# Chosen rows of the last gated layer go to the output by indirect, accumulating transfers

## The reference, cut to what matters

```python
x = x + attn_a(layernorm(x), Wq, Wk, Wv, Wo)            # causal, 16 heads of 16
x = x + ffn(layernorm(x), Wg, Wq, Wk, Wv, Wo)           # gated attention, "layer 1"
x = x + attn_b(layernorm(x), w_qkv, w_out, rel_bias)    # 16 heads of 64, with a bias
x = x + ffn(layernorm(x), Wg, Wq, Wk, Wv, Wo)           # the same gated attention, "layer 3"

def ffn(t):                       # t: 8 x 512 x 256
    gate = sigmoid((t @ Wg)[..., 0])
    _, idx = top_k(gate, 256)                           # 256 of 512 tokens of each sample
    a = take_along_axis(t, idx[..., None], axis=1)
    q, k, v = heads(a @ Wq), heads(a @ Wk), heads(a @ Wv)
    o = merge(softmax(q @ k.T / sqrt(16)) @ v) @ Wo
    out = zeros_like(t)
    out[rows, idx] = o * take_along_axis(gate, idx, axis=1)[..., None]
    return out
```

## Time and profile before

| | |
|---|---|
| median of 3 runs | 2024.09 us (2023.55 to 2024.71) |
| profiled execution | 2022.95 us, span 2020.9 us |
| PE, PE weight loads, VectorE, ACT, GpSimd busy | 98%, 63%, 75%, 57%, 34% |
| granted TensorE clock, share of full speed | 0.998 |
| transfers | 14.9% of 16 engines' time, 49 GB/s of HBM over the span |

### The profile page before, as it was taken

The page is one execution under the profiler, slowest core; times in us unless marked ns, Lnnn a source line. Parts: engine busy times, 40 slices in busy tenths (PEclk is TensorE's granted clock), DMA queues, the critical chain, the costliest instruction groups (busy, mean ns, idle before and its releaser), DMA issues.

```text
span 2020.9 us, 41852 instructions
## 1 busy us (share of the span) xinstructions
PE 1970.7 (98%) x15934; PEld 1264.9 (63%) x15934; DVE 1518.8 (75%) x4803; ACT 1158.5 (57%) x2578; POOL 690.7 (34%) x879
## 2 busy tenths in 40 slices
PE   8999999999999999999999999999999999999998
PEld 6566665666665666656666566655666566666577
DVE  8987767767877778868779687796787967856536
ACT  2455674575637765376644757367663576627642
POOL 5323234242333323433324324234233342313320
PEclk9999999999999999999999999999999999999999
DMA  4001221111201121111211112011120111102200
GB/s 170 2 1 35 78 79 46 46 54 35 84 27 54 46 73 46 45 36 63 74 37 35 54 46 83 29 53 54 42 78 19 61 54 41 68 16 72 76 6 11
DMA packets 31078, 102.42 MB, mean 51 GB/s; under 512 B 3105, under 2 KB 11425, under 8 KB 30753
## 3 DMA queue, kind: packets, MB, share of 16 engines
q1 hardware_dynamic: 30880, 99.76, 14.9%
HBM read 95.56 MB, written 4.19 MB: 49 GB/s over the span
## 4 chain that ended last, share of the span: by engine, by line
PE 76%; DVE 19%; ACT 3%; issue 1%; POOL 0%; DVEq 0%
PE ps L959 21%; PE ps L1711 11%; PE ps L1693 11%; PE ps L1701 9%; PE ps L1472 6%; DVE ps L1327 5%; PE ps L1555 3%; PE ps L1660 3%; PE ps L1569 3%; PE ps L1648 3%; DVE probs L1418 2%; PE ps L1626 2%; PE ps L1531 2%; DVE peaks L1401 1%; DVE stats L1247 1%
## 5 line engine op out<-in xcount | busy, mean ns | idle before, releaser
L1132 POOL TENSOR_SCALAR probs<-probs,rtotal 128x512 f32<-128x512 f32 x512 | 353.7, 709 | 651.3 <-DVE rtotal L1427 650.5
L1223 ACT ACTIVATE probs<-probs,peak 128x512 f32<-128x512 f32 x512 | 365.3, 714 | 152.5 <-DVE peak L1423 152.3
L1418 DVE CUSTOM_DVE_ANT_0 probs<-ps,band 128x512 f32<-128x512 f32 x512 | 332.7, 687 | 70.7 <-PE ps L1693 70.1
L1232 ACT ACTIVATE PT<-ps 128x512 f32<-128x512 f32 x512 | 266.5, 620 | 56.7 <-PE ps L1701 55.4
L1701 PEld LDWEIGHTS ps<-ident,probs 128*128 128x128 f32 x2048 | 225.7, 141 | 48.9 <-issue 38.9
L1701 PE MATMUL ps<-ident,probs 128*128 128x128 f32 x2048 | 249.9, 274 | 3.5 <-DVE peaks L1327 2.8
L1327 DVE CUSTOM_DVE_ANT_0 ps<-ps,later 128x512 f32<-128x512 f32 (+3 forms) x512 | 232.8, 525 | 13.6 <-PE ps L1531 12.7
L1693 PE MATMUL ps<-KT,QT 64*128 64x512 f32 x1024 | 242.2, 606 | 0.4
L1711 PE MATMUL ps<-PT,Vb 128*64 128x512 f32 x1024 | 237.1, 600 | 0.0
L959 PE MATMUL ps<-xnT,wb 128*128 128x512 f32 x512 | 234.8, 601 | 2.4 <-DVE peak L1418 1.7
L1196 ACT ACTIVATE PTc<-ps 128x384 f32<-128x384 f32 (+1 forms) x384 | 168.8, 553 | 70.0 <-PE ps L1555 69.4
(11 more groups left out here) (156 smaller groups left out, 3302.5 us busy)
## 6 DMA issues: line engine op xcount, KB each, us to landing
band<-in_band SPq DMA_DIRECT2D x64, 896.0 KB, 4.6
wb<-in_w_b SPq DMA_DIRECT2D x64, 384.0 KB, 3.1
x<-in_x SPq DMA_DIRECT2D x16, 256.0 KB, 3.1
out<-x SPq DMA_DIRECT2D x16, 256.0 KB, 2.2
cos<-in_cos SPq DMA_DIRECT2D x8, 256.0 KB, 2.7
sin<-in_sin SPq DMA_DIRECT2D x8, 256.0 KB, 3.0
wob<-in_wo_b SPq DMA_DIRECT2D x1, 1024.0 KB, 9.1
wqk<-in_wqk_a SPq DMA_DIRECT2D x1, 512.0 KB, 5.6
```

Of the source, the lines that this page charges most:

```text
L1132: last = g.tensor_scalar(unit, unit, rtotal[:, r % 8, e:e + 1], 1.0, ALU.mult, ALU.mult)
L1223: last = a.activation(unit, unit, ACT.Exp, bias=peak[:, r % 8, e:e + 1], accum_out=total[:, r % 8, e:e + 1])
L1232: a.activation(PT[:, k % 2, e, :, tile_of(q)], bank(now, name).rearrange("p (k n) -> p k n", k=NT), ACT.Copy).then_inc(act_read, 1)
L1418: v.tensor_tensor_reduce(out=probs[:, (r + LENT) % ROWS_HELD, e, :], in0=bank(now, name), in1=band[:, k % 2, e, lo:lo + T], scale=1.0, sca ...
```

## The change

In layer 3 the result is no longer brought back to the tokens on chip. The output gets x as it is after layer 2, by plain stores behind b_y. Then f_sc (f_o's matmuls, under a new name) leaves the 256 result rows in PSUM, ACT writes them to `of`, scaled by their gates, and f_add has GpSimd start two indirect transfers of 128 rows each that add the rows to the output at their tokens' places. The addresses and gates of the chosen tokens come from a new step f_idx in place of f_spread: eight fp32 matmuls of `pick` with `marks`, two columns that hold each token's number and its gate. It waits for `pick`, where f_spread waited for the rank alone. f_spread, of_hi, of_lo and both f_y go, in layer 3 only. ACT's copy in the next f_gather waits for the transfers, since `of` and `xgT` share memory. Every other step keeps the place that it had in the order, though most of PLACE's numbers are written anew. The gates now lie two apart in memory.

```diff
+    "f_idx": [("o", "dve", 1)], "f_sc": [("o", "act", 1)],
...
+    "f_idx": [("pe", 0.6), ("dve", 0.15), ("dve", 0.15)],
+    "f_sc": [("pe", 1.729), ("act", 0.35), ("act", 0.35)],
+    "f_add": [("pool", 1.3), ("pool", 1.3)],
...
-    ("cycle3", "f_gather"): [4788],
-    ("cycle3", "f_o"): [5462],
-    ("cycle3", "f_spread"): [4769],
-    ("cycle3", "f_y"): [5536, 5361],
-    ("last1", "f_gather"): [22421],
-    ("last1", "f_spread"): [6974],
-    ("last2", "f_y"): [22508, 24703],
+    ("cycle3", "f_gather"): [4861],
+    ("cycle3", "f_sc"): [5354],
+    ("cycle3", "f_idx"): [4824],
+    ("cycle3", "f_add"): [5203],
+    ("last", "b_y"): [22614, 21438, 21443, 21563],
+    ("last1", "f_gather"): [24487],
+    ("last1", "f_idx"): [24318],
+    ("last2", "f_gather"): [20259],
+    ("last2", "f_idx"): [17168],
+    ("last2", "f_add"): [22614],
...
-    late = [Step("f_y", s - 3, 3, 1)] if s >= 3 else []
+    late = [Step("f_ln", s - HELD, 3)] if s >= HELD else []
...
+    if l == 3:
+        return out + [(f("sc"), [f("vb", 0), f("vb", 1), f("idx")], []), (f("add"), [f("sc")], [])]
...
-                        if kind == "f_y" and l == 3:
+                        if kind == "b_y" and q == 1:
                             sp.wait_ge(dve_read, plan.unit(now, now))
                             two = slice(2 * n, 2 * n + 2)
                             sp.dma_start(ov[s][:, two], x[:, s % HELD, two]).then_inc(x_stored[s % HELD], 16)
-                            if n == 1:
-                                sp.wait_ge(x_stored[s % HELD], 32 * (s // HELD + 1))
-                                if s + HELD < B:
-                                    load_x(sp, s + HELD)
+                        if kind == "f_rank" and l == 3 and s + HELD < B:
+                            sp.wait_ge(xn_done, plan.after("xn", Step("f_ln", s, l), now))
+                            sp.wait_ge(x_stored[s % HELD], 32 * (s // HELD + 1))
+                            load_x(sp, s + HELD)
+                    sp.wait_ge(out_added, 32 * B)
...
+                    for some in marks:
+                        g.iota(some[:, :, 0], pattern=[[P, NT]], base=0, channel_multiplier=1,
                                allow_small_or_imprecise_dtypes=True).then_inc(consts, 1)
...
+                        if kind == "f_add":
+                            pool.wait_ge(x_stored[s % HELD], 32 * (s // HELD + 1))
+                            pool.wait_ge(dve_read, plan.unit(Step("f_idx", s, l), now))
+                            pool.wait_ge(act_read, plan.unit(Step("f_sc", s, l), now))
+                            for j in range(NS):
+                                g.indirect_dma_start(out_rows, bass.IndirectOffsetOnAxis(m.token[:, j:j + 1], 0), m.of[:, j, :], None,
+                                                     bounds_check=B * T - 1, compute_op=ALU.add).then_inc(out_added, 16)
...
+                        if kind == "f_sc":
+                            act.wait_ge(dve_read, plan.unit(Step("f_idx", s, l), now))
+                            for j in range(NS):
+                                last = a.activation(m.of[:, j, :], bank(now)[:, j * D:(j + 1) * D], ACT.Copy,
+                                                    scale=m.gate_sel[:, j:j + 1])
+                            last.then_inc(act_read, 1)
                         if kind == "f_gather":
+                            old = plan.latest(now, "f_add")
+                            if old is not None:
+                                at_least(act, out_added, 32 * plan.after("added", old, now))
...
+                        if kind == "f_idx":
+                            found = bank(now)[:, 0:2 * NS].rearrange("p (j k) -> p j k", k=2)
+                            v.tensor_scalar(m.token, found[:, :, 0], float(T * s), None, ALU.add)
+                            v.tensor_copy(m.gate_sel, found[:, :, 1]).then_inc(dve_read, 1)
...
+                        if kind == "f_idx":
+                            at_least(pe, consts, CONSTS)
+                            pe.wait_ge(pick_done, plan.after("pick", Step("f_rank", s, l), now))
+                            room(now)
+                            for j in range(NS):
+                                last = product(o[:, 2 * j:2 * j + 2], [(m.pick[:, t, tile_of(j)].bitcast(F32), m.marks[:, t, :])
+                                                                       for t in range(NT)])
+                        if kind in ("f_o", "f_sc"):
```

More of the change, by code:

```diff
@@ L93 @@
     "norm": {"b_nrm": 1},
+    "added": {"f_add": 1},
 }
@@ L204 @@
 PLACE = {
[L205 to L211, removed]
@@ L240 @@
[L240 to L254, removed]
@@ L282 @@
[L282 to L285, removed]
-        3344, -378, 2447, 3164, 2704, 1887, 2378, 3227, -10239, -1785, -695, 1184, 3089, 3430, 2564, 2052],
@@ new lines @@
+    ("cycle", "f_part"): [-284],
+    ("cycle", "f_q"): [196],
+    ("cycle", "f_rank"): [26],
+    ("cycle", "f_row"): [-49],
+    ("cycle", "f_rq"): [-424],
+    ("cycle", "f_spread"): [122],
+    ("cycle", "f_v"): [264],
+    ("cycle", "f_va"): [400, 459],
+    ("cycle", "f_vb"): [-20871, 404],
+    ("cycle", "f_xq"): [297],
+    ("cycle", "f_y"): [602, -2491],
+    ("cycle3", "f_gate"): [4705],
+    ("cycle3", "f_gather"): [4861],
+    ("cycle3", "f_hk"): [1502],
+    ("cycle3", "f_hm"): [4009, 5208],
@@ new lines @@
+    ("first0", "c_y"): [811, -480],
+    ("first0", "f_gate"): [-1222],
+    ("first0", "f_gather"): [1127],
+    ("first0", "f_hk"): [38],
+    ("first0", "f_hm"): [870, -27],
+    ("first0", "f_k"): [833],
+    ("first0", "f_ln"): [866],
+    ("first0", "f_m"): [1258, 1395],
+    ("first0", "f_o"): [1501],
+    ("first0", "f_p1"): [1229, 1193, 1265, 1254],
+    ("first0", "f_p2"): [768, 1319, 278, -930],
+    ("first0", "f_part"): [-56],
+    ("first0", "f_q"): [550],
+    ("first0", "f_rank"): [1040],
@@ new lines @@
+    ("first1", "f_gate"): [1527],
+    ("first1", "f_gather"): [1648],
+    ("first1", "f_hk"): [969],
+    ("first1", "f_hm"): [622, 1084],
+    ("first1", "f_k"): [1826],
+    ("first1", "f_ln"): [269],
+    ("first1", "f_m"): [2103, 2465],
+    ("first1", "f_o"): [2964],
+    ("first1", "f_p1"): [-150, 2084, 1907, 2097],
+    ("first1", "f_p2"): [2352, 2226, 2085, 362],
+    ("first1", "f_part"): [-684],
+    ("first1", "f_q"): [1837],
+    ("first1", "f_rank"): [1563],
+    ("first1", "f_row"): [-218],
@@ new lines @@
+    ("first1", "f_rq"): [549],
+    ("first1", "f_spread"): [2960],
+    ("first1", "f_v"): [1848],
+    ("first1", "f_va"): [2521, 2802],
+    ("first1", "f_vb"): [1808, 1093],
+    ("first1", "f_xq"): [1897],
+    ("first1", "f_y"): [3120, 2576],
+    ("last", "b_k"): [-1335, 20445, 20288, 20662, 20610, 21416, 21615, 21406],
+    ("last", "b_ln"): [20053],
+    ("last", "b_nrm"): [19874, 20288, 20367, 20312, 21269, 19913, 20028, 20189, 20631, 20631, 20237, 18466, 21405,
+        20006, 20956, 21483, 21402, 19024, 20278, 20740, 19246, 21406, 21405, 21507, 21411, 20644, 21406, 16321, 21717,
+        5492, 21840, 20783],
```

382 lines of the change are left out of this document (178 added, 204 removed).

## The result

The changed kernel takes 2038.22 us (median of 4 runs, 2035.21 to 2038.75) against 2024.18 us for the kernel before, run beside it: 14.0 us slower, ratio 1.0067, 95% interval 1.0054 to 1.0081. The forecast was 2022.6 us and its range ended at 2030. The profiled execution took 2038.27 us, with a span of 2036.5 us. Times of runs are medians; two of the ten runs of e8 took 4952.7 and 5839.8 us, more than twice as long as the others, and are left out.

The account below looks back on a forecast made before the run. TensorE's queue order was taken to bound samples 0 to 5, and waits and a chain across engines samples 6 and 7. Terms -2.8 + 0.7 + 1.8 - 1.2 = -1.5 us off 2024.09 gave 2022.6 us, range 2012.5 to 2030.

Parts of the forecast that it names:

- samples 0 to 5: Steady samples where TensorE's queue sets the time: -0.57 us each plus 0.1 lost at f_row, -2.8 us for six.
- samples 6 and 7: Last two samples: +0.7 us in sample 6, and +1.8 us in sample 7 for f_idx between pick and f_gather.
- the tail: From the last scalings to the end: 6.0 us instead of 7.2, -1.2 us, with bounds of -3.0 and +3.6.
- f_idx's price: TensorE's cost for the new f_idx: sixteen loads at 0.111 us plus 0.14 for entering, 1.92 us a sample.
- Rival A: f_idx costs only 0.6 us, as in the planner's table: 9.4 us less, 2013.2 us; chance 0.2.
- The step that failed first: After f_y's place: VectorE's score reads, GpSimd's normalising and the gate all come some 0.8 us sooner.
- f_y's 1.91 us: Sixteen spreading matmuls removed from TensorE in each sample, expected back almost whole, with 0.1 us lost at f_row.
- rival C: Norm or gate isn't sooner, so f_y's time becomes a TensorE wait: +1.3 us a sample, 2033 us; chance 0.1.
- the bank choice: Warning that the planner's new choice of banks opens waits elsewhere: 0.5 us a period would be 3 us.
- GpSimd's queue: Two indirect issues at 1.3 us each hide in 5.8 us of GpSimd's idle time ahead of b_nrm: no cost.
- Rival B: An indirect issue takes 3.5 us, making b_nrm late and TensorE wait at b_tr: 2034 us; chance 0.1.

Follow-up runs that it names:

- e8: Changed kernel's work in the old kernel's order, f_idx moved behind f_v, no idle transposes in the steady periods; 2027.93 us, ratio 1.0020 to the kernel before.
- e1: Changed kernel's work with every step in the order of the kernel before; 2032.93 us, ratio 1.0048 to the kernel before.
- e10: Changed kernel, its order and idle transposes kept, with f_idx alone in fp32r; 2031.19 us, ratio 1.0040 to the kernel before.
- e7: e8 with f_idx in fp32r, half the pairs of load and matmul; 2020.12 us, ratio 0.9986 to the kernel before.
- e3: Kernel before with seven of the eight matmuls of each last-layer f_y left out; 2016.51 us, ratio 0.9966 to the kernel before.
- e6: Old work in the changed kernel's order, without idle transposes in the steady periods; 2032.14 us, ratio 1.0038 to the kernel before.
- e4: Changed kernel with f_idx moved from ahead of the gather to right behind f_v, rest of the order as it is; 2038.27 us.
- e5: Changed kernel without the idle transposes of the steady periods; 2037.43 us.
- e2: Kernel before, its old work put in the changed kernel's order; 2037.00 us, ratio 1.0061 to the kernel before.
- e9: e8 with the indirect transfers of samples 0 to 6, and ACT's wait for them, left out; 2028.82 us.

## Why the prediction was wrong
The record's sum, laid over the columns of the table: it had -2.8 us for samples 0 to 5, and A with five periods came out at +6.3; it had +2.5 for samples 6 and 7, and E came out at +8.7; it had -1.2 for the tail, and T came out at +0.6.

**f_idx's price was right.** The sum had sixteen loads at 0.111 us and 0.14 for entering, 1.92 us. In the chain in order of time, the way in which f_spread's 0.58 was read, f_idx and f_gather take 3.70 us in the changed kernel and 3.88 in e1, and f_gather alone 1.92 before: 1.78 and 1.96 for f_idx. Halving the pairs took 0.9 us off (e10, e7), 0.11 a pair. Rival A fell with it. The rule that stood beside it, of the Trainium skill, page TensorE: Matmul & The Clock Gate, section Weight-path perf modes, is that Fast Weight Load is on only where the input isn't FP32. The traces agree for fp32: 0.11 us a pair against the 24 ns of the bf16 steps. In fp32r a pair still took 0.11 (e10) to 0.13 us (e7).

**The step that failed first** is "VectorE loses its wait for of_hi and of_lo itself, so its eight reads of scores ... start some 0.8 us sooner". They started 0.15 us sooner behind the ACT instruction of that place (1.16 against 1.31 us). Of_lo had not been the only thing ahead of them: TensorE releases the first bank of scores only some 1.3 us after its first matmul. In the changed kernel's timeline VectorE starts the first read at that release, and TensorE fills the wait for the gate with idle transposes:

```profile
988.25 0.84 ACT L1224 ACTIVATE of<-ps,gates_sel 128x256 f32<-128x256 f32 x2 [1.02 <-PE ps L1507]
989.41 0.69 DVE L1454 CUSTOM_DVE_ANT_0 probs<-ps,band 128x512 f32<-128x512 f32 x1 [3.25 <-PE ps L1735]
...
995.51 2.69 POOL L1155 TENSOR_SCALAR probs<-probs,rtotal 128x512 f32<-128x512 f32 x4 [2.02 <-DVE rtotal L1463]
...
1002.06 0.88 PE L1527 MATMUL ps<-ident 128*128 128x128 f32 x6
1002.24 0.18 DVE L1398 RECIPROCAL marks<-z 128x4 f32<-128x4 f32 x1
...
1002.77 0.60 PE L1617 MATMUL ps<-ident,marks 128*128 128x128 f32 x4
```

Behind the reads hangs one chain: VectorE's reciprocal, GpSimd's b_nrm, GpSimd's rstd of the next gated layer, VectorE's norm, the gate. With the reads it stayed where it was: b_nrm starts 995.51 - 988.25 = 7.26 us behind the ACT instruction instead of 7.39 (7.61 in e8), and the gate is 1002.42 - 988.25 = 14.17 us behind instead of 14.29.

What that costs TensorE is read best in e8, whose steps in this stretch stand where the kernel before has them, and which has no idle transposes:

```profile
997.81 2.71 POOL L1307 TENSOR_SCALAR probs<-probs,rtotal 128x512 f32<-128x512 f32 x4 [2.38 <-DVE rtotal L1615]
...
1000.57 1.10 PE L1895 MATMUL ps<-ident,probs 128*128 128x128 f32 x8 [0.25 <-POOL probs L1307]
...
1004.79 0.65 PE L1769 MATMUL ps<-ident,marks 128*128 128x128 f32 x4 [0.35 <-DVE marks L1550]
```

All of f_y's 1.91 us is there when TensorE reaches b_tr, 7.89 us behind the ACT instruction at 990.20 instead of 9.80. It loses 0.8 of it there: the third row is ready only when GpSimd ends at 1000.52, 10.3 us behind where the record counted on 9.3, and b_tr takes 3.5 us instead of 2.7. At f_row it loses another 0.4, waiting for the gate. So 0.7 of 1.91 us came back. In e1 b_tr is the same, but six idle transposes stand ahead of f_row, 0.7 is lost there, and 0.4 came back. (e3, without the rest of the change, shows 0.8 of 1.67.) With f_idx less f_spread, 1.96 - 0.58 = 1.38 us, e1's 0.4 leaves 1.0, and its period grew by 1.04; e8's 0.7 leaves 0.7, and its period grew by 0.6. That is rival C, by its mechanism: it had a chance of 0.1 and was sized at 1.8 us a sample above the forecast, and the changed kernel's period came out 1.5 above the forecast's 241.6. The changed kernel's period grew by 1.06 us, as e1's, but its steps stand in another order and were not followed one by one. The record also warned of the bank choice, which is made anew in every kernel here; no run holds it fixed, and e1's sum leaves it less than 0.1 us a period.

**The order.** That all else stays in place was taken from the words of the change, and the list was not worked out. With the new work it cost nothing in the periods (e1 and the changed kernel, 243.1 both; both have six idle transposes there); with the old work it cost 1.07 us (e6). The two effects don't add. In samples 6 and 7 the new order cost 2.8 us with the old work (e6 against before) and 2.9 with the new one (e4 against e8, which also differ in one group of six idle transposes).

**The clock** was no term at all. In sample 6 it cost 4.4 us, between rows that are alike in both kernels. It fell there in both profiles that had a full f_idx ahead of the gather in the new order (the changed kernel, e5), and not when f_idx was moved (e4), halved (e10) or absent (e2, e6), nor in e1, where the same rows stood; each of these is one profile. Which detail decides it was not found. The run of the changed kernel at a mean clock of 0.998 took 2035.21 us, 11 us over before; by this one run about 3 of the 14 us go with the clock.

**Samples 6 and 7.** f_idx ahead of the gather costs its full 1.8 us in each, as the record has it: in sample 6 e1 needs 8.3 us from f_idx to the scores behind the projections, and the kernel before, from f_gather to the same place, 6.5 (1808.91 to 1815.42). In sample 7 of the changed kernel it is 4.55 us from f_idx to f_k, and before, from f_gather, 2.86. With 4.4 for the clock, 2.8 for the order and two f_idx less f_y's 1.1 these terms add to 9.7, one more than E grew; they overlap.

**The tail.** Scalings 0.84 (0.82 forecast), hand-over 0.87 (0.1), two issues 1.55 + 0.30 + 1.54 = 3.4 (2.6), and then 2.7 to the end, of the forecast's 2.5. The failed terms are the hand-over from ACT to GpSimd and the issue, 1.55 instead of 1.3 us with a gap of 0.3; the sum is 7.8, within the record's bounds.

**GpSimd's queue** was right: 1.65 + 0.31 + 1.56 us of issue end 2.0 us before b_nrm starts at 995.51, and e9 shows that the period does not depend on them. Rival B did not happen. The warning that the record named beside it, of the Trainium skill, page SBUF — State Buffer, section Who interferes with whom (descriptors of a GpSimd DMA starved by VectorE's 2-port modes), has no trace here: an issue beside a busy VectorE took 1.65 and 1.56 us, at the end beside an idle one 1.55 and 1.54. Whether VectorE was in such a mode beside them is not shown.

## What to carry to other kernels
Before counting what TensorE no longer does as a gain, follow the chain through the other engines to the next step that TensorE needs from them: only the slack in front of that step comes back, here 0.4 to 0.7 of 1.9 us. Work out the order of both kernels when a table of places changes, whatever the text says, and look at what the program derives from it, such as idle transposes. Judge an edit of a few microseconds by a steady stretch of the trace, since the whole holds spells of half clock that come and go between executions of one kernel.

## What the runs showed of the hardware
- An indirect transfer with accumulate, 128 rows of 1 KB, keeps GpSimd 1.61 us (mean of 16, 1.54 to 1.79), with 0.3 us between two. It landed 3.6 to 4.1 us from its issue, and the second of each pair in samples 0 to 5 after 6.7 to 7.0 us (why is not shown), against a median of 2.2 for a plain store of 256 KB. At the end it starts 0.87 us after ACT's last scaling ends.
- A matmul with 128 fp32 weight columns and two moving ones costs its load, 0.11 us, and fp32 takes two a product (1.78 us for sixteen in e8); in fp32r, with four moving columns, a product takes one (1.06 us for eight in e7).
- TensorE's clock went to the lower level for 3.4 to 17 us at 106 to 112 us of the span in most of the profiled executions. It stayed up in the changed kernel's, whose steps up to there are e4's (17.1 us low); TensorE had waited 0.61 and 1.7 us just before in both.
